# A hand-ordered four-layer graph network on one core: all engines' step orders and PSUM banks laid out anew

## The chip, the cores and the metric

The kernel runs on one core of a Trainium2 chip. The core has a matrix engine (TensorE, "PE" in the profile, with its weight loads on a line of their own, "PEld"), VectorE (DVE), ScalarE (ACT), GpSimd (POOL) and SyncE (SP, which here only issues DMAs). They run apart from each other and meet at semaphores. TensorE writes its results only to PSUM, which has 8 banks of 512 fp32 columns per partition; the other engines read them from there. The metric is device microseconds of one execution of the whole program, as a median over runs.

## The reference

x is 32 graphs of 512 nodes with 128 features, adj one 512x512 0/1 matrix for all of them. Four layers follow each other, each on a normalised and clipped input, and each added to x:

```python
h = jnp.maximum(_layernorm(x, axis=-1), 0.0)
x = x + _L0_gnn_ref(h, adj, ...)     # attention from a fixed pairing of nodes, softmax over axis 1, + h @ self_weight
h = jnp.maximum(_layernorm(x, axis=-1), 0.0)
x = x + _L1_gnn_ref(h, adj, ...)     # attention, layernorm, adj @ h, MLP with layernorm, residual, relu
h = jnp.maximum(_layernorm(x, axis=-1), 0.0)
x = x + _L2_gnn_ref(h, adj, ...)     # attention, + bias, elu
h = jnp.maximum(_layernorm(x, axis=-1), 0.0)
x = x + _L3_gnn_ref(h, adj, ...)     # softmax(edge values) @ h W1, the diagonal @ h W0, + bias
```

An attention of layers 1 and 2 is softmax over the neighbours of leaky_relu(s_i + t_j), and then a product with the features. Everything is fp32. The 32 graphs do not depend on each other; layer 3's 512x512 matrix is made once, from adj.

## The kernel before

**Tiling.** The 32 graphs are taken two at a time: 16 groups, numbered 0 to 15, in the kernel's tables 0 to 9 and a to f. A group's x is 128 partitions x 8 rows x 128. Six slots (NS = 6) hold the buffers of the groups in flight; group g uses slot g modulo 6. A setup block loads weights and adj, and an own chain of twelve "prep" steps (table name g) makes layer 3's matrix while the first groups run.

**Steps.** The table STEPS cuts the work of a group into 55 steps, and says for each how many PSUM tiles it opens and which engines have a part in it. One layer goes round the engines in a long loop: `stat` (VectorE takes the layernorm statistics, L1143; GpSimd makes 1/sqrt of them, L1066 to L1081), `scale` (ScalarE applies it, eight instructions of L921), `norm` (TensorE turns the rows, L634; ScalarE moves them out of PSUM into HT, L914 or L912), and then the layer's products. The steps that the texts below speak of:

- `norm0`, `coef0`, `cmax0`, `coefb0`, `feat0`, `agg0`, `self0`: layer 0. `coef0` is the group of narrow products with wcols; `feat0` the products with Wo.
- `feat1`, `top1`, `spread1a/b`, `att1a/b`: layer 1's features, the maximum turned through TensorE (L732, read by VectorE L1260), the row factors spread through TensorE (L741, from ScalarE's CE, L944), and the attention product (VectorE makes PT, L1280; TensorE multiplies it with HE). The same steps with a 2 are layer 2's; `sums2` is a small product beside them.
- `gin1`, `mlpa1`, `mlpb1`, `mlpc1`: the product with adj, the two MLP products and the layernorm between them. After `mlpc1` VectorE makes the new x (L1311, L1315).
- `elu2`: layer 2's end. `norm3`, `feat3`, `agg3`: layer 3, whose result goes out by DMA.

**What sets the order.** No engine chooses anything when the program runs. The table TURNS holds one string for each engine: each character is a group, and that group's next step on this engine stands next. The function `walk` emits them in that order:

```python
for e, turns in TURNS.items():
    todo = [(name for name, _, engines in steps if e in engines.split()) for steps in [STEPS] * GROUPS + [PREP]]
    order[e] = [(int(g, GROUPS + 1), next(todo[int(g, GROUPS + 1)])) for g in turns]
```

So an engine that comes to a step whose input isn't there waits, and all steps behind it wait with it. The table HOMES gives, in TensorE's order, the bank of each PSUM tile that a step opens (895 of them):

```python
for g, name in order["pe"]:
    for n in range(tiles_of[name]):
        bank = int(next(home))
        tile_at[name, g, n] = bank, opened[bank]
```

TensorE opens a tile only when the one before it in that bank has been read (`open_tile`, semaphore `taken`); the readers wait for `full`. The inner content of each step is fixed. TensorE has 471 steps in its string, VectorE 472, ScalarE 404, GpSimd 144, SyncE 32 loads and stores.

Of the kernel before, what the change touches and what calls it, by code (L numbers as in the profile page):

```python
# [118 lines left out]
    ("eturn", 4, "pe act dve"),  # L119
]  # L120
TURNS = {
    "pe": ("gggggg1021000011201022110g20000001311324331121103024422341401035224121020004300330021112135013332111"
           "5024504434422225432142223163551434333563353325644226755645534446446344563578866776566547648847555855"
           "565576988a9a999777857877a68758865997887696666aa66687897abb9a8bb9989976777776776b899888ba88b889cc977c"
           "c7b9889999c9899dbbccbbdaabcedbec9cdcc9ceed9bcbddfeaafbbeaaeddfcdfddecbdbbbfdbbebbeaffcddeecafbbefdfb"
           "ffcecccdccffcdceeadddafddfeddcaceffacaaeaaeeaeafdeedeedffaffafffeaeefff"),
    "act": ("gg01201200g11002g00301102344110011530223011224010141510022300032421301231201102233103342544322153224"
           "46132314463434553334722346255744365534445583646558566574496645765685556a5869a79875877566977a58877769"
           "88766668897867a8bb88996b79976777a689978b99888ac99c8777b9889b8c999cdd9bbecbceaab99cc9dbbcedbbcffbbeca"
           "caddbecddeafbcdbbbcdfabdadeedcfdbbfabdecffdceccceaffddefceefaddefdfaccdeffcadeeaaafeeefdadeaafffaefe"  # L130
           "efff"),
    "dve": ("g0g12gggg100000102111002g111g00300422501123211022013334304212134410403224311002403400223000112335113"
           "1110322305441644225553222422133544155273433363355633424255866644546664554433457496678665576477468756"
           "58a5855558776888599997777aa889758877669995b8667668a8a666a6897a9b7aab99889777767799bbb67889bc88bb7888"
           "998c77c899d9cc899c9eb9bcccbada9bdebcccc9ebb9dddfbcdddeeeaabcbeeefcafddddacbbffbbedfabbbedfdffbeedccb"
           "afffbeccfddccfeeccfcedfdcaadddfdddeecaffcaaaeaeaeedaaeeedffeffaffffeeaff"),
    "pool": ("012001102134502231043140324102032511653435247234668356594475678a87895569a76987ba867a896bb9cb77988cdc"
           "ec99bddfbecedbeafcdffbbdcaedfeaccfdefdaaeeff"),
    "sp": ("102354061728394a5b6c7d8e9fbcdeaf"),
}  # L140
HOMES = ("0123456701234567012345670125634701254637542601375401430751430051430571426573014303014265742654276534"
         "2703142657203165410365471203654715240365402713617543062175435473535470621062130547210631054726310572"
         "6310573141057341703535326264170532170654321706543706521064375210640641375264026402640264026401375261"
         "3761524037615261403765240314031765231407652314310765210761076152076152431531024224531052376410524371"
         "6052437160541603703754167037272720372037524160375160537124605371242453712736045162730451645451654165"
         "4162730162730162730301627301627301630154623701375460123754601234760513476205132040432510432325104327"
         "6105432761207651423075075076570142365736501426501420650627350736250723560516474207542160754235342160"
         "7416241076262641057324612461246120547631542073616157432061574342061576123547546102735410276413502764"
         "1354135410273641573641502020273641502152150736421642156073421560734215607347340215671340256713456713"
         "450")  # L150


def bcast(ap, n):
# [14 lines left out]
def gnn_kernel(nc, x, adj, Wo_d, Ws_d, att0_d, Wp_d, bp_d, asrc_d, adst_d, gatg_d, gatb_d, eps_d, W1_d, b1_d,  # L168
# [12 lines left out]
    with ctx:  # L181
# [61 lines left out]
        tile_at, mat_at, mat_of = {}, {}, []  # L243
        opened, home = [0] * BANKS, iter(HOMES)
        for g, name in order["pe"]:
# [1266 lines left out]
```

How the kernel before makes its waits and increments, by code:

```python
            @block.sync  # L428
            def _(sp):
                for t in range(T):
                    sp.dma_start(adj_raw[:, t, :], adj[t * P:(t + 1) * P, :]).then_inc(adj_loaded, 16)
                for dst, src in LOADS[0::2]:
                    sp.dma_start(dst, src).then_inc(loaded, 16)
                for s in range(NS // 2):
                    for b in range(G):
                        sp.dma_start(X[s][:, b::G, :],
                                     x.rearrange("b (t p) f -> b p t f", p=P)[s * G + b]).then_inc(x_loaded[s], 16)
                for s in taken:
                    sp.sem_inc(s, 1)
                for s in sig["stored"]:
                    sp.sem_inc(s, 16)
                sp.wait_ge(loaded, 16 * len(LOADS[0::2]))
# [1 line left out]
            @block.gpsimd  # L445
            def _(pool):
                nc.gpsimd.memset(ident[:], 0.0).then_inc(made["pool"], 1)
                nc.gpsimd.memset(ones[:], 1.0).then_inc(made["pool"], 1)
                nc.gpsimd.memset(work1[:], 1.0).then_inc(made["pool"], 1)
                nc.gpsimd.memset(minus_half[:], -0.5).then_inc(made["pool"], 1)
                nc.gpsimd.memset(ones_r[:].bitcast(F32), 1.0).then_inc(made["pool"], 1)
                pool.wait_ge(made["pool"], 5)
                nc.gpsimd.affine_select(out=ident[:], in_=ident[:], compare_op=ALU.not_equal, fill=1.0, base=0,
                                        pattern=[[-1, P]], channel_multiplier=1).then_inc(made["pool"], 1)
```

## Time and profile before

| | |
|---|---|
| median of 3 runs | 1142.54 us (1142.05 to 1143.92) |
| profiled execution, its own time | 1142.13 us |
| its span in the trace | 1140.1 us, 21695 instructions |
| TensorE matmuls busy | 1012.0 us, 89% of the span |
| TensorE weight loads busy | 959.3 us, 84% |
| VectorE busy | 862.8 us, 76% |
| ScalarE busy | 632.3 us, 55% |
| GpSimd busy | 473.3 us, 42% |
| mean granted clock of TensorE | 0.94 of full |
| DMA | 20.20 MB, 18 GB/s on average |

Busy time is the time in which an engine had an instruction under way. TensorE's matmuls overlap, so their time is no measure of how many would fit; the weight loads on their own line say more about that. A bracket behind an instruction of the timeline is the idle time of its engine just before it, and who ended it. The granted clock is one of two levels, 1.0 (2.4 GHz) and 0.5 (1.2 GHz); a value between them is a mean over a stretch.

### The profile page before, as it was taken

What the parts mean: (1) busy time and instruction counts of PE and PEld (TensorE: products, weight loads), DVE (VectorE), ACT (ScalarE), POOL (GpSimd) and SP (SyncE); (2) the same over time, 40 slices, a digit from 0 to 9 for tenths busy, and PEclk for the clock granted to TensorE, in tenths of its full rate; (3) what the DMA queues carried; (4) which work ended last, traced back from release to release, by engine and by line L of the source; (5) the groups of instructions that cost most, each with busy time, mean ns of one, the idle gap of its engine ahead of it and who ended that gap; (6) DMA issues with size and microseconds to landing.
All of it is one profiled execution on the core that took longest, in us unless ns stands there. A gap on an engine that the chain in (4) does not pass through costs nothing. (4 is left out here: it accounts for less than half of the span.)

```text
span 1140.1 us, 21695 instructions
## 1 busy us (share of the span) xinstructions
PE 1012.0 (89%) x7611; PEld 959.3 (84%) x7611; DVE 862.8 (76%) x2536; ACT 632.3 (55%) x1647; POOL 473.3 (42%) x1134
## 2 busy tenths in 40 slices
PE   2597899989899989899999999899999989898997
PEld 2586788979798889889888989789989989888986
DVE  3769777876877668688686988859678876787874
ACT  1053667665565655463645685564655656667352
POOL 2123543643354334443425551633345344546132
PEclk7688799999999889899799999899999999999999
DMA  5000100000101010110001001011010000000001
GB/s 127 1 1 1 56 1 2 1 1 1 37 2 38 1 38 1 38 38 1 1 1 38 1 2 39 1 38 38 1 38 1 1 1 19 2 1 20 2 19 56
DMA packets 38491, 20.20 MB, mean 18 GB/s; under 512 B 3184, under 2 KB 37872, under 8 KB 38384
## 3 DMA queue, kind: packets, MB, share of 16 engines
q1 hardware_dynamic: 36512, 18.42, 5.8%
q8 instruction: 61, 1.00, 0.4%
q10 hardware_dynamic: 1872, 0.40, 0.2%
q14 instruction: 46, 0.38, 0.1%
HBM read 10.43 MB, written 8.39 MB: 17 GB/s over the span
## 5 line engine op out<-in xcount | busy, mean ns | idle before, releaser
L617 PE MATMUL ps<-HE,PT 128*128 128x129 f32 x2048 | 261.2, 280 | 6.0 <-issue 5.0
L617 PEld LDWEIGHTS ps<-HE,PT 128*128 128x128 f32 x2048 | 247.7, 196 | 7.6 <-issue 6.8
L921 ACT ACTIVATE Y<-X,SM 128x128 f32<-128x128 f32 x512 | 203.3, 489 | 54.1 <-POOL SM L1081 54.0
L1280 DVE SCALAR_TENSOR_TENSOR PT<-ps,CE,maskT 128x512 f32<-128x512 f32 x256 | 174.2, 743 | 46.0 <-PE ps L741 39.9
L1066 POOL TENSOR_TENSOR SM<-ST 128x8 f32<-128x8 f32 x96 | 25.9, 270 | 380.0 <-DVE ST L1143 380.0
L1077 POOL TENSOR_TENSOR SM<-SM,minus_half 128x8 f32<-128x8 f32 x96 | 164.6, 1714 | 7.6
L617 PE MATMUL ps<-W,HT 128*128 128x128 f32 (+1 forms) x768 | 133.7, 324 | 3.4 <-ACT HT L914 3.1
L617 PEld LDWEIGHTS ps<-W,HT 128*128 128x128 f32 x768 | 121.4, 202 | 14.8 <-ACT HT L914 4.0
L1143 DVE BATCH_NORM_STATS2 ST<-X 128x6 f32<-128x128 f32 x512 | 104.6, 278 | 17.4 <-DMA X<-in_x_dram 14.8
L634 PE MATMUL ps<-ident,Y 128*128 128x128 f32 x640 | 85.5, 280 | 18.2 <-ACT Y L921 17.5
L634 PEld LDWEIGHTS ps<-ident,Y 128*128 128x128 f32 x640 | 73.2, 145 | 22.2 <-ACT Y L921 20.2
L914 ACT ACTIVATE HT<-ps 128x512 f32<-128x512 f32 x96 | 52.1, 600 | 58.8 <-PE ps L634 58.7
L1098 POOL TENSOR_TENSOR LOWB<-HE,HIB 128x1024 fp32r<-128x1024 f32 x16 | 36.4, 2276 | 110.1 <-ACT HIB L938 110.1
L617 PE MATMUL ps<-HI,a_hi 128*128 128x256 f32 x256 | 74.2, 290 | 4.5 <-DVE LOW L1447 4.5
L617 PE MATMUL ps<-HI,a_lo 128*128 128x256 f32 x256 | 72.8, 284 | 0.0
L617 PE MATMUL ps<-LOW,a_hi 128*128 128x256 f32 x256 | 72.6, 284 | 0.0
L955 ACT ACTIVATE HE<-ps,HE 128x128 f32<-128x128 f32 x256 | 68.9, 380 | 0.0
L617 PE MATMUL ps<-gin_hi,LOW 128*128 128x512 f32 x128 | 57.8, 452 | 3.8 <-DVE LOW L1299 2.7
L1103 POOL TENSOR_TENSOR X<-X,bias 128x1024 f32<-128x1024 f32 x16 | 38.5, 2409 | 54.4 <-ACT Y L921 54.4
L921 ACT ACTIVATE HE<-Y,SM 128x128 f32<-128x128 f32 x128 | 51.1, 492 | 16.5 <-POOL SM L1081 16.4
L921 ACT ACTIVATE Y<-Y,SM 128x128 f32<-128x128 f32 x128 | 51.1, 497 | 12.1 <-POOL SM L1081 12.1
L1143 DVE BATCH_NORM_STATS2 ST<-Y 128x6 f32<-128x128 f32 x256 | 51.7, 275 | 5.7 <-ACT Y L986 5.0
(265 smaller groups left out, 2385.4 us busy)
## 6 DMA issues: line engine op xcount, KB each, us to landing
X<-in_x_dram SPq DMA_DIRECT2D x32, 256.0 KB, 3.4
out_dram<-X SPq DMA_DIRECT2D x32, 256.0 KB, 2.8
adj_raw<-in_adj_dram SPq DMA_DIRECT2D x4, 256.0 KB, 3.8
W<-in_L_gnn_W_dram SPq DMA_DIRECT2D x1, 128.0 KB, 4.3
Ws<-n_L_gnn_self_weight_dram ACTq DMA_DIRECT2D x1, 64.0 KB, 3.4
W<-in_L_gnn_W_dram ACTq DMA_DIRECT2D x1, 64.0 KB, 3.8
feat2w<-in_L_gnn_W_dram ACTq DMA_DIRECT2D x1, 64.0 KB, 4.4
Wo<-L_gnn_others_weight_dram SPq DMA_DIRECT2D x1, 64.0 KB, 4.6
```

The lines of the kernel that those rows point to most:

```text
L617: return nc.tensor.matmul(o, w, m, start=start, stop=stop, skip_group_check=True)
L634: mm = T_(o[:, t * P:(t + 1) * P], Y[s][:, t * G + b, 0:F], ident[:])
L914: a = A(HT[s][:, b, :], o, ACT.Relu)
L921: a = A(dst[:, n, 0:F], src[:, n, 0:F], func, scale=SM[s][:, S_RSTD, n:n + 1], bias=SM[s][:, S_SHIFT, n:n + 1])
L955: a = A(HE[s][:, k, 0:F], o[:, 2 * P * b:2 * P * b + F], ACT.Identity, scale=HE[s][:, k, F:F + 1])
L1066: TT(sm[:, S_DIF, :], st[:, :, 1], st[:, :, 4], ALU.subtract)
L1077: link(TT(sm[:, S_RSTD, :], sm[:, S_VAR, :], minus_half[:], ALU.pow))
L1098: TT(LOB[s], VA[s], HIB[:].bitcast(F32), ALU.subtract).then_inc(sig["by_pool"][s], 1)
L1103: TT(X[s][:], X[s][:], repeat(bias3[:], TG), ALU.add).then_inc(sig["by_pool"][s], 1)
L1143: a = V.bn_stats(ST[s][:, n, :], src(n))
L1280: a = V.scalar_tensor_tensor(out=PT[r][:, j, :], in0=o, scalar=CE[s][:, c:c + 1], in1=maskT[:, j, :].bitcast(F32), op0=ALU.max, op1=ALU.mult)
```

## The change

Only the two tables are new: TURNS (the order of the steps on each engine) and HOMES (the bank of each tile). The steps, their contents, their instructions, the buffers and all waits that follow from the data stay; a wait for a bank follows its new neighbour. On TensorE 342 of 471 steps stand at another place, by 1.7 places on average and by 15 at most; on VectorE 352 of 472 (1.6 on average, at most 10), on ScalarE 299 of 404, on GpSimd 78 of 144, and 9 of the 32 loads and stores. TensorE's first eight steps and the last three are the same. The diff (cut; the rows of both tables are all replaced in this manner):

```diff
 TURNS = {
-    "pe": ("gggggg1021000011201022110g20000001311324331121103024422341401035224121020004300330021112135013332111"
+    "pe": ("gggggg1001001021120011g20002020010131231213341103420224434101032421520120030400300323123113151311125"
...
-    "sp": ("102354061728394a5b6c7d8e9fbcdeaf"),
+    "sp": ("135024061728394a5b6c7d8e9fadbcef"),
 }
-HOMES = ("0123456701234567012345670125634701254637542601375401430751430051430571426573014303014265742654276534"
+HOMES = ("0123456701234567012345670123456710456273410627341056267234105467235726435107210764325107643762435763"
...
```

**TensorE, layer 2 of group 6.** The rows below are `feat2` (feat2w,HT), `sums2` (feat2w,HS), `top2` (ident,MX), `spread2a` and `spread2b` (ident,CE) of group 6, with steps of other groups between them. Before:

```order
L634 MATMUL ps<-ident,Y 128x128 x16
L617 MATMUL ps<-feat2w,HT 128x130 x8
L617 MATMUL ps<-feat2w,HS 128x128 x2
L732 MATMUL ps<-ident,MX 128x128 x2
L741 MATMUL ps<-ident,CE 128x128 x4
L617 MATMUL ps<-Wo,HT 128x128 x8
L617 MATMUL ps<-CS,adj_top 128x4 x8
L741 MATMUL ps<-ident,CE 128x128 x4
```

And now, the same place (bias,pick and W,HT are `mlpa1` of group 7):

```order
L617 MATMUL ps<-feat2w,HT 128x130 x8
L617 MATMUL ps<-feat2w,HS 128x128 x2
L732 MATMUL ps<-ident,MX 128x128 x2
L617 MATMUL ps<-bias,pick 128x512
L617 MATMUL ps<-W,HT 128x128 x4
L617 MATMUL ps<-bias,pick 128x512
L617 MATMUL ps<-W,HT 128x128 x4
L741 MATMUL ps<-ident,CE 128x128 x8
```

`spread2a` stood right behind `top2`; now the MLP step of another group stands between them.

**TensorE, layer 0 of groups 9 and 10.** The rows are `norm0` (ident,Y), `coef0` (wcols,HT), `cmax0` (ident,MX) and `feat0` (Wo,HT), the first row the end of group 8's `self0`. Before:

```order
L617 MATMUL ps<-Ws,HT 128x128 x4
L634 MATMUL ps<-ident,Y 128x128 x8
L617 MATMUL ps<-wcols,HT 128x4 x16
L725 MATMUL ps<-ident,MX 128x128 x2
L617 MATMUL ps<-Wo,HT 128x128 x8
```

And now:

```order
L617 MATMUL ps<-Ws,HT 128x128 x4
L617 MATMUL ps<-wcols,HT 128x4 x8
L634 MATMUL ps<-ident,Y 128x128 x8
L725 MATMUL ps<-ident,MX 128x128 x2
L634 MATMUL ps<-ident,Y 128x128 x8
L617 MATMUL ps<-Wo,HT 128x128 x8
L617 MATMUL ps<-wcols,HT 128x4 x8
```

The two groups' `coef0`, 16 narrow products in a row before, stand apart.

**VectorE, behind `mlpc1` of group 7.** L1315 is the last instruction of `mlpc1`, which makes the group's new x; the L1143 on X that belongs to it is `stat2` of the same group. Before:

```order
L1311 SCALAR_TENSOR_TENSOR Y<-HE,ps 128x4x128 x2
L1315 SCALAR_TENSOR_TENSOR X<-Y,X 128x1024
L1224 SCALAR_TENSOR_TENSOR X<-ps,CE,X 128x128 x8
L1260 TENSOR_REDUCE MX<-ps 128x2
L1264 TENSOR_TENSOR CF<-DS,MX 128x8
L1266 TENSOR_SCALAR CF<-DS,MX 128x4 x2
L1155 COPY US<-ps 128x32
L1158 COPY CD<-US 128x8
L1159 TENSOR_TENSOR CD<-US 128x4
L1161 SCALAR_TENSOR_TENSOR CD<-CD 128x12
L1163 TENSOR_REDUCE MX<-CD 128x2
L1143 BN_STATS ST<-X 128x6 x8
```

And now:

```order
L1311 SCALAR_TENSOR_TENSOR Y<-HE,ps 128x4x128 x2
L1315 SCALAR_TENSOR_TENSOR X<-Y,X 128x1024
L1143 BN_STATS ST<-X 128x6 x8
L1280 SCALAR_TENSOR_TENSOR PT<-ps,CE,maskT 128x512 x4
L1143 BN_STATS ST<-Y 128x6 x8
L1280 SCALAR_TENSOR_TENSOR PT<-ps,CE,maskT 128x512 x4
L1224 SCALAR_TENSOR_TENSOR X<-ps,CE,X 128x128 x8
```

The statistics stand right behind the new x; three steps of other groups that stood between them (`agg0`, `top1`, `coef0`) have gone to other places.

## Rows read from the trace of the kernel before

**Rows 1.** The page, busy time of the engines (us, share of span, instructions).

```profile
PE 1012.0 (89%) x7611; PEld 959.3 (84%) x7611; DVE 862.8 (76%) x2536; ACT 632.3 (55%) x1647; POOL 473.3 (42%) x1134
```

**Rows 2.** Busy time by stretch: length, engines with instructions, granted clock, DMA share, GB/s.

```profile
0.00:38.60 38.60, 7.75 (x31) 6.91 (x31) 19.52 (x70) 5.63 (x7) 7.92 (x14) 0.71 0.44 94
38.60:68.00 29.40, 26.97 (x108) 22.73 (x109) 18.19 (x54) 12.46 (x30) 10.87 (x30) 0.74 0.00 1
68.00:1140.00 1072.00, 977.33 (x7473) 929.65 (x7471) 825.12 (x2414) 614.18 (x1611) 454.50 (x1090) 0.95 0.05 15
```

**Rows 3.** Waits of TensorE from 68 us on: total us, times, longest.

```profile
PE ps L634 <- ACT Y L921: 17.5, 11, 6.1
PE ps L741 <- ACT CE L944: 11.5, 10, 1.4
PE ps L732 <- DVE MX L1254: 11.3, 15, 2.1
PE ps L617 <- ACT HT L914: 7.6, 9, 1.2
PE ps L617 <- ACT HT L912: 4.6, 4, 1.5
PE ps L617 <- DVE LOW L1299: 2.7, 3, 1.8
```

**Rows 4.** Timeline of TensorE, steps that stood right behind their source: start, us, instruction.

```profile
127.27 7.92 PE L617 MATMUL ps<-HE,PT 128*128 128x129 f32 x46 [3.04 <-issue]
...
392.07 0.47 PE L617 MATMUL ps<-bias,pick 128*128 128x512 f32 x1 [1.15 <-ACT HT L910]
...
506.23 2.02 PE L617 MATMUL ps<-feat2w,HT 128*128 128x130 f32 x16 [0.96 <-ACT HT L912]
...
618.30 0.65 PE L741 MATMUL ps<-ident,CE 128*128 128x128 f32 x4 [1.33 <-ACT CE L944]
...
736.36 5.38 PE L617 MATMUL ps<-W,HT 128*128 128x256 f32 x16 [0.78 <-ACT HT L914]
...
781.98 0.43 PE L732 MATMUL ps<-ident,MX 128*128 128x128 f32 x2 [0.46 <-DVE MX L1254]
```

**Rows 5.** Timeline of TensorE, `feat0` at half and at full clock.

```profile
547.95 3.62 PE L617 MATMUL ps<-Wo,HT 128*128 128x128 f32 x16
...
618.79 1.95 PE L617 MATMUL ps<-Wo,HT 128*128 128x128 f32 x16
```

**Rows 6.** Busy time by stretch, the two `coef0` of groups 9 and 10 and after.

```profile
545.60:559.20 13.60, 12.87 (x60) 12.50 (x61) 6.62 (x29) 8.92 (x24) 7.76 (x23) 0.50 0.00 0
559.20:600.00 40.80, 38.11 (x290) 34.89 (x289) 31.46 (x84) 21.01 (x58) 14.73 (x38) 1.00 0.01 2
```

**Rows 7.** Timeline, group 7 from `mlpc1` to `norm2`, all engines.

```profile
642.58 1.05 PE L617 MATMUL ps<-W,HT 128*128 128x128 f32 x8
...
646.69 1.23 DVE L1315 SCALAR_TENSOR_TENSOR X<-Y,X 128x1024 f32<-128x1024 f32 x1
647.95 2.29 DVE L1224 SCALAR_TENSOR_TENSOR X<-ps,CE,X 128x128 f32<-128x128 f32 x8
...
652.04 1.64 DVE L1143 BATCH_NORM_STATS2 ST<-X 128x6 f32<-128x128 f32 x8
...
659.14 3.21 ACT L921 ACTIVATE Y<-X,SM 128x128 f32<-128x128 f32 x8
...
662.42 3.21 ACT L921 ACTIVATE Y<-X,SM 128x128 f32<-128x128 f32 x8
...
668.53 0.71 PE L634 MATMUL ps<-ident,Y 128*128 128x128 f32 x5
```

**Rows 8.** Timeline of GpSimd, the power instruction twice.

```profile
646.69 2.75 POOL L1077 TENSOR_TENSOR SM<-SM,minus_half 128x8 f32<-128x8 f32 x1
...
651.78 1.68 POOL L1077 TENSOR_TENSOR SM<-SM,minus_half 128x8 f32<-128x8 f32 x1
```

**Rows 9.** The page, the group of the power instruction (mean in ns of one).

```profile
L1077 POOL TENSOR_TENSOR SM<-SM,minus_half 128x8 f32<-128x8 f32 x96 | 164.6, 1714 | 7.6
```

More of the change, by code:

```diff
@@ L121 @@
 TURNS = {
-    "pe": ("gggggg1021000011201022110g20000001311324331121103024422341401035224121020004300330021112135013332111"
[L123 to L130, printed above, removed]
-           "efff"),
[L132 to L136, printed above, removed]
@@ L137 @@
-    "pool": ("012001102134502231043140324102032511653435247234668356594475678a87895569a76987ba867a896bb9cb77988cdc"
-           "ec99bddfbecedbeafcdffbbdcaedfeaccfdefdaaeeff"),
-    "sp": ("102354061728394a5b6c7d8e9fbcdeaf"),
-}
-HOMES = ("0123456701234567012345670125634701254637542601375401430751430051430571426573014303014265742654276534"
[L142 to L150, printed above, removed]
@@ new lines @@
+    "pe": ("gggggg1001001021120011g20002020010131231213341103420224434101032421520120030400300323123113151311125"
+           "4020404324422425235422213135513633453463533643524526625457345446443644565368676865647757846457555988"
+           "5655576889a979a9877a57877878659865988676667669aa668b9b978799aa979b878677b7767b7869888988bb88a9c79cb7"
+           "cc7898999cb99899cdbcbdaebbcadbc9cecac9dd9cebcbadeedfbabeefdadbdcdebdbcfbdbbffdebbaeffcedcdafbefbfefe"
+           "cfbdcccdcfcfccdadeddeddfafeddecfacfaaaceadeaeeaeeafdffefedaffafefeaefff"),
@@ new lines @@
+    "act": ("gg0110201g2010g0200101320311404015132023012142010141102503203100220321321311243021400332442532422345"
+           "13123146334635454334246235524743736554443585645565866454674965758695655568a67a7988577a59687765877686"
+           "89766679887b86ba7899679879867b77698987b98898ac7989cb7a7b8989c8999cd9debbecbc9abad9cc9bbcedbcbfbbefdc"
+           "bdaacebddceabcfbbdadfcdbadeecdfbfdbabfecedcfdccefcaefddcafefddedfeefcafdcafcdaeaeadeeeffdfaffeaaaeef"
+           "efff"),
+    "dve": ("g12g0gggg0011001010100g121g2010030242215102312102031334302214143410043232114020400202303033412101115"
+           "3112023435410442262355242252133545543123433635673544233562566844564466545443534666768795574867747565"
+           "685a558558778889956a9977a78798758696758799b8666768a8a66699ab677989aaa97b87876779bb976778b8c89b8bb888"
+           "899c7c7899ccdb9899ce9c9bccb9dabadccbc9edb9bceddfacbdeaddeebbeeecfcdaddbdfbacbffdbbaefbdbedfffbcceefb"
+           "fdfeafbccddcecfccecdcfdfeddaafddeddecafacaefeaaeeadafafeeeeffdaffffeefaf"),
@@ new lines @@
+    "pool": ("120010102132405231304103412240032513156435422674386536547495678a878956a5796987ba6789b68ba7c97b898ccd"
+           "ec9d9bedfbcdebeafcfdfbbcdeadfecafcdefdaeaeff"),
+    "sp": ("135024061728394a5b6c7d8e9fadbcef"),
+}
+HOMES = ("0123456701234567012345670123456710456273410627341056267234105467235726435107210764325107643762435763"
+         "2471605320547146057132460571324163167243167240524052430167526752675674230156715674230542637105423710"
+         "5423716130754230617615764230764230157642031576420315764215767036703670421561356135615361750426175325"
+         "3613761304250425761034253425342537615034276742150376124576103576035716024731560601512473547360541273"
+         "6054127360451260457345126047303470370370531264317026574031572640263157402316457026341571571450721634"
+         "5340721653402170217026534065342065201734652065201736420517364207364732051632407512407512407070512643"
+         "2436243636243627405135165136513652740427136541365036503764150372645021645163701263701237645014052376"
+         "1452054250437612506123742374237504621375042137163507142614261426142635104726372632651074263510742634"
+         "2364251074326514307265143075126430751075107264531031725604316072543416130472651472630514307265143075"
+         "143")
```

## The prediction

> **What bounds the kernel now.** I read the busy times first: TensorE's matmuls 89% of the span, its weight loads 84%, VectorE 76%, ScalarE 55% [rows 1]. Then the same by stretch [rows 2]. Up to 38.6 us the setup runs, and from there to 68 us TensorE does prep work in an order that the change leaves alone. The change can act on the remaining 1072 us only. There TensorE has 977.3 us of matmuls, so it is idle for 94.7 us, at a mean granted clock of 0.95; VectorE is busy for 825.1 us, 77%. TensorE is the bound in the middle, but it waits about 9% of the time. The waits [rows 3] are of two sorts. Short ones: the step that stands next on TensorE needs what VectorE or ScalarE makes of the step just before (CE from L944, MX from L1254, HT from L914 and L912). Long ones: the first product of a new layer (L634 behind ACT Y L921) comes before the loop through VectorE, GpSimd and ScalarE is round; 17.5 us in 11 waits. The chain that ends last is made of TensorE's work and of these waits, so whatever is taken from them is taken from the time, as long as nothing else comes late.
>
> By a rule of the Trainium skill (Perfetto Trace Analysis, Identifying the Most-Contended Engine) matmul time overstates how full TensorE is, and weight load time says it better. The trace has 929.7 us of weight loads in the 1072 [rows 2], so by the rule the room is 142 us and not 95; the sum below doesn't use it.
>
> **The change, part by part.** No instruction is added or removed, so nothing has to be priced but order. I price it by neighbours on TensorE.
>
> *Short round trips.* For each pair of steps of one group in which the second needs the answer of another engine to the first, I take the shortest idle time that the trace shows with nothing between them: top to spread 1.33 us, mlpb1 to mlpc1 1.15, norm2 to feat2 0.96, norm3 to feat3 0.78, feat1 to top1 0.46, spread to attention about 3.0 [rows 4]; the others (feat3 to agg3, norm0 to coef0, coef0 to cmax0, gin1 to mlpa1 and so on) are read in the same way. Against it stands the TensorE work between the two in either order, each step at the shortest time that it took in the trace. Where the work is shorter than the trip, TensorE must wait for the difference. Counting places that lack at least 0.25 us:
>
> before there are 54 with 48.6 us in all, after there are 17 with 12.2 us. The largest items: top2 to spread2a 6 places and 7.1 us, then none; spread to attention 7 and 6.9 us, then 4 and 3.0; feat1 to top1 9 and 4.1 us, then 3 and 1.4; mlpb1 to mlpc1 3 and 3.4 us, then none; norm3 to feat3 4 and 3.1 us, then 1 and 0.8; norm2 to feat2 3 and 2.9 us, then none. Group 6 shows how: its spread2a waited 1.33 us behind top2 [rows 4], and now mlpa1 of group 7 stands between, whose two tiles take longer than that (a later mlpc1 half, 8 matmul records of the same form, takes 1.05 us [rows 7]). The waits bear the count out: those of the short sort by L944, L1254, L914 and L912 alone come to 35.0 us [rows 3]. The difference is 36.4 us; about 1.4 us of it I count twice (coefb0 is followed by both agg0 and self0), so −35. Lower end: half of it, −18, if the step put between is itself late as often as not; upper end −36.
>
> *Long loops.* Five trips go through three engines: self0 to norm1, att1b to gin1, mlpa1 to mlpb1, mlpc1 to norm2, att2b to norm3. By the same count with the shortest loop of each kind they lack 27.4 us before and 30.7 after, so +3.3 as one end. But most loops were longer than the shortest. With each group's own loop of before, up to the end of the ScalarE or VectorE instruction that TensorE waits for, the 80 loops lack 175 us before and 256 after: the new order brings their ends 81 us closer in all. Group 7's mlpc1 to norm2 is the plainest. Its loop was 22.0 us long: mlpc1 ends at 643.6 [rows 7], the last L921 of scale2 at 665.6, and TensorE began norm2 at 668.53. Now only 10.7 us of TensorE work stand between. The other engines' orders are changed to suit. On VectorE three steps of other groups stood between L1315, which ended at 647.9, and the statistics at 652.04 (4.1 us); they are gone from there. On ScalarE scale2 ran at 662.42 behind another scale [rows 7]; that one stays. So this loop falls to about 18 us, and lacks 7 of them. Such a shortage is not a wait of the same size, since the groups of six slots are in flight and delay each other's steps only once: in the trace 175 us of shortage go with 17.5 + 2.7 = 20.2 us of waits [rows 3], which makes +9 of the 81; divided by six groups in flight it makes +14. I take +14, the dearer, because group 7 keeps 7 us. Other end: half of 81, +40.
>
> *Clock.* At half clock the 16 matmuls of feat0 take 3.62 us, at full 1.95 [rows 5], so 46% of such a time is lost. With 0.95 over 1072 us [rows 2] some 107 us run at half, and 107 x 0.91 x 0.46 is 45 us. The longest stretch, 13.6 us, lies behind the two coef0 in a row of groups 9 and 10 [rows 6], and these stand apart now. Others followed TensorE's idle places. But the long waits will make new ones, so I take a tenth of the 45, −4; ends 0 and −15.
>
> *Banks.* A tile now waits for another tile's reader. In the order before, a twentieth of the tiles were opened within 0.85 us of work behind the tile before them in the bank; in the new one within 1.54. No wait of before names a bank with more than 1 us, so the gain is put at nothing (ends 0 and −2), covered by other waits at the same places. The loads and stores that moved are nothing: 9 of 32, and SyncE is idle in between.
>
> *Sum.* Own time of the profiled execution 1142.1; −35 + 14 − 4 = −25 gives 1117.1. The median is 0.4 above the profiled time, so 1117.5.
>
> **The rivals.**
>
> 1. *The loops get shorter too.* If VectorE and ScalarE run everywhere as behind mlpc1 of group 7, the long term is +3.3 and the clock gives −15: −36 + 3 − 15 = −48, 1094. For it: both engines have room (77% and 57% of the 1072 us [rows 2]), and the tables of all engines were changed together. Against: a loop that lacks 7 us.
>
> 2. *The waits only move.* TensorE finds its next input sooner, but VectorE in its fixed order is late instead, and the short gains end in front of the next step. Then 1141. For it: VectorE is at 77%, and a late step there holds whatever stands behind it. Against: the waits on VectorE's L1254 and L1299 are under 2.2 us each [rows 3].
>
> 3. *Slower: the tight loops.* If the loops keep their length and each group's lateness holds up the next, the long term is half of the 81, +40.5; with −35 and no clock gain that is +5.5, 1148. It decides from the point where the long term passes 35 + 2.3. It would show first at norm2 of group 7 (10.7 us for a loop of 22.0) and at gin1 of group 6. For it: the sum is real and has nothing to hide it but idle room of others. Against: 175 us of shortage cost only 20 before.
>
> 4. *GpSimd is held up.* The power instruction took 1.68 us mostly and 2.75 when it met VectorE work [rows 8], 1.07 more. A new order has new meetings. If each of the 96 rstd chains met one, 96 x 1.07 / 6 in flight is +17 over the forecast: 1134. But the mean of all 96 power instructions is 1.71 [rows 9], so few of them meet anything now, and I give it little.
> The Trainium skill (SBUF — State Buffer, Who interferes with whom) has the rule behind such a case: VectorE with two inputs in SBUF and GpSimd share one pair of ports, and the one that comes second waits for the whole instruction. The trace agrees by that 1.07 us.
>
> **How the numbers follow.** Forecast 58% (1107 to 1130), rival 1 20%, rival 2 7%, rival 3 9%, rival 4 6%. The range of 8 in 10 reaches from 1095, which takes in half of rival 1 and a little more, to 1141, which leaves out rival 3 and a part of rival 2. About 0.2% (2.3 us) is what can be told from no change here. Faster by more: forecast, rival 1, rival 4 and a little less, 0.83. Within: most of rival 2, 0.07. Slower: rival 3 and the rest, 0.10.
>
> **What would show it.** In the changed profile, TensorE's waits on L944, L1254, L914 and L912 should fall from 35.0 to about 10 us, and spread2a of group 6 should start without an idle time. TensorE's waits on ACT Y L921 should rise from 17.5 to some 30. The idle time behind 68 us should go from 94.7 to about 73, and the granted clock stay at 0.95 or rise a little. Matmul durations at full clock must be the same. I am wrong if the short waits stay above 25 us (then the steps put between are late themselves), if L921 waits pass 50 us (rival 3), or if the clock alone moves the time by more than 15 us.

## The result, and the profile after

The kernel after takes 1085.06 us (median of 4 runs, 1079.57 to 1088.0) against 1143.23 for the kernel before beside it: 0.9479 of its time, 95% interval 0.9431 to 0.9526. The forecast was 1117.5 us with a range of 1095 to 1141. The direction was right; the gain is more than twice the size, 58 us for a forecast 25.

The profiled execution took 1079.57 us, the fastest of the four; its span is 1077.8. Busy times of the page, the answer to [rows 1]:

```profile
PE 985.5 (91%) x7611; PEld 940.4 (87%) x7611; DVE 857.4 (80%) x2536; ACT 634.1 (59%) x1647; POOL 482.6 (45%) x1134
```

The same by stretch, the answer to [rows 2] (length, then TensorE, its weight loads, VectorE, ScalarE, GpSimd, the granted clock, DMA share, GB/s):

```profile
0.00:38.60 38.60, 7.76 (x31) 6.92 (x31) 19.14 (x67) 5.63 (x7) 7.92 (x14) 0.71 0.53 94
38.60:68.00 29.40, 26.16 (x106) 22.00 (x107) 18.27 (x56) 9.87 (x22) 10.40 (x30) 0.74 0.00 1
68.00:1077.80 1009.80, 951.57 (x7476) 911.53 (x7474) 820.02 (x2415) 618.60 (x1618) 464.25 (x1090) 0.97 0.06 16
```

All of it is behind 68 us: that part fell from 1072.0 to 1009.8, by 62.2 us. It splits in two. Idle TensorE time went from 94.7 to 58.2 (−36.5). Matmul time went from 977.3 to 951.6 (−25.8), with the same instructions. This second part the forecast had at 4 us.

The waits of TensorE from 68 us on (total us, times, longest), the answer to [rows 3]:

```profile
PE ps L634 <- ACT Y L921: 14.9, 12, 3.6
PE ps L617 <- ACT HT L914: 4.7, 5, 1.8
PE ps L732 <- DVE MX L1254: 4.1, 6, 1.6
PE ps L741 <- ACT CE L944: 2.7, 4, 1.4
...
PE ps L617 <- ACT HT L912: 1.2, 1, 1.2
...
PE ps L617 <- DVE LOW L1299: 0.8, 2, 0.5
```

The four short ones (L944, L1254, L914, L912) fell from 35.0 to 12.7 us, close to the 10 of the forecast. The long one behind L921 should have risen to 30 and fell from 17.5 to 14.9.

Group 6 on TensorE, the answer to the fourth row of [rows 4]: behind `top2` (ident,MX) stands `mlpa1` of group 7, and `spread2a` (ident,CE) starts without idle time. The step put between waits 0.52 us itself, so 0.8 of the 1.33 us are won here.

```profile
574.87 0.43 PE L732 MATMUL ps<-ident,MX 128*128 128x128 f32 x2
575.83 0.47 PE L617 MATMUL ps<-bias,pick 128*128 128x512 f32 x1 [0.52 <-ACT HT L981]
576.14 1.05 PE L617 MATMUL ps<-W,HT 128*128 128x128 f32 x8
576.95 0.48 PE L617 MATMUL ps<-bias,pick 128*128 128x512 f32 x1
577.27 1.05 PE L617 MATMUL ps<-W,HT 128*128 128x128 f32 x8
578.16 1.04 PE L741 MATMUL ps<-ident,CE 128*128 128x128 f32 x8
```

Group 7 from `mlpc1` to `norm2`, the answer to [rows 7]:

```profile
606.90 1.05 PE L617 MATMUL ps<-W,HT 128*128 128x128 f32 x8
607.75 1.39 DVE L1311 SCALAR_TENSOR_TENSOR Y<-HE,ps 128x512 f32<-128x512 f32 x2
609.18 1.23 DVE L1315 SCALAR_TENSOR_TENSOR X<-Y,X 128x1024 f32<-128x1024 f32 x1
610.44 1.65 DVE L1143 BATCH_NORM_STATS2 ST<-X 128x6 f32<-128x128 f32 x8
...
616.59 0.20 POOL L1081 TENSOR_TENSOR SM<-SM 128x8 f32<-128x8 f32 x1
616.82 3.19 ACT L921 ACTIVATE Y<-X,SM 128x128 f32<-128x128 f32 x8 [0.78 <-POOL SM L1081]
...
620.07 1.09 PE L634 MATMUL ps<-ident,Y 128*128 128x128 f32 x8 [1.12 <-ACT Y L921]
```

`mlpc1` ended at 607.95, `norm2` began 12.1 us later; before it was 24.9. The statistics start 0.03 us behind the new x instead of 4.1. From the end of `mlpc1` to the end of `scale2` this loop takes 12.1 us (607.95 to 620.01), where the forecast gave it 18. `scale2` still follows another group's scale on ScalarE, as the forecast said, but that one (612.86 to 616.05, `scale3` of group 6) is done before this group's factors are ready, and costs it nothing. Against the 10.7 us of TensorE work between, a loop of 12.1 lacks 1.4, and the wait is 1.12: the forecast's way of counting holds here, its length of the loop does not.

At full clock matmuls take what they took: the 16 of `feat0` 1.95 us, as in [rows 5]. What is new is how long the clock is full. From the trace's records of the granted clock TensorE ran at half for 99.0 us before, and for 51.2 after, from 68 us to its last matmul. Both are of one execution each, and this time varies from one execution to the next: the mean granted clock lay between 0.934 and 0.961 in 19 runs of the kernel before, and between 0.948 and 0.967 in the 4 of the kernel after. The page's group of the power instruction, the answer to [rows 9], hardly moved (1714 to 1699 ns):

```profile
L1077 POOL TENSOR_TENSOR SM<-SM,minus_half 128x8 f32<-128x8 f32 x96 | 163.1, 1699 | 7.6
```

### The profile page after: what moved, and what is told of

Same layout as the page of the kernel before. It is cut to its first block and busy times, and to the rows that moved or that the text cites. A ratio compares the mean times of both kernels' runs of the same rounds, so it can differ in the third digit from the quotient of the medians.

```text
span 1077.8 us, 21695 instructions
## 1 busy us (share of the span) xinstructions
PE 985.5 (91%) x7611; PEld 940.4 (87%) x7611; DVE 857.4 (80%) x2536; ACT 634.1 (59%) x1647; POOL 482.6 (45%) x1134
## 5 line engine op out<-in xcount | busy, mean ns | idle before, releaser
L617 PE MATMUL ps<-HE,PT 128*128 128x129 f32 x2048 | 257.5, 277 | 2.1 <-issue 1.6
L617 PEld LDWEIGHTS ps<-HE,PT 128*128 128x128 f32 x2048 | 243.8, 193 | 3.0 <-issue 2.4
L921 ACT ACTIVATE Y<-X,SM 128x128 f32<-128x128 f32 x512 | 203.5, 485 | 70.7 <-POOL SM L1081 70.6
L1066 POOL TENSOR_TENSOR SM<-ST 128x8 f32<-128x8 f32 x96 | 23.7, 247 | 336.8 <-DVE ST L1143 336.6
L1077 POOL TENSOR_TENSOR SM<-SM,minus_half 128x8 f32<-128x8 f32 x96 | 163.1, 1699 | 7.6
L617 PE MATMUL ps<-W,HT 128*128 128x128 f32 (+1 forms) x768 | 127.1, 313 | 0.8 <-ACT HT L914 0.8
L617 PEld LDWEIGHTS ps<-W,HT 128*128 128x128 f32 x768 | 116.1, 194 | 10.4 <-ACT HT L914 1.0
L1143 DVE BATCH_NORM_STATS2 ST<-X 128x6 f32<-128x128 f32 x512 | 104.7, 278 | 5.2 <-DMA X<-in_x_dram 2.2
L634 PE MATMUL ps<-ident,Y 128*128 128x128 f32 x640 | 86.4, 282 | 15.4 <-ACT Y L921 14.9
L634 PEld LDWEIGHTS ps<-ident,Y 128*128 128x128 f32 x640 | 74.2, 146 | 19.4 <-ACT Y L921 17.9
L921 ACT ACTIVATE HE<-Y,SM 128x128 f32<-128x128 f32 x128 | 51.1, 486 | 25.8 <-POOL SM L1081 25.8
L914 ACT ACTIVATE HT<-ps 128x512 f32<-128x512 f32 x96 | 51.5, 595 | 22.8 <-PE ps L634 22.4
L921 ACT ACTIVATE Y<-Y,SM 128x128 f32<-128x128 f32 x128 | 51.0, 490 | 15.9 <-POOL SM L1081 15.9
L1143 DVE BATCH_NORM_STATS2 ST<-Y 128x6 f32<-128x128 f32 x256 | 51.5, 274 | 9.8 <-ACT Y L986 8.9
L617 PEld LDWEIGHTS ps<-HI,a_hi 128*128 128x128 f32 x256 | 48.6, 190 | 4.1 <-DVE LOW L1447 3.2
```

What stands on the lines that cost most here:

```text
L617: return nc.tensor.matmul(o, w, m, start=start, stop=stop, skip_group_check=True)
L634: mm = T_(o[:, t * P:(t + 1) * P], Y[s][:, t * G + b, 0:F], ident[:])
L914: a = A(HT[s][:, b, :], o, ACT.Relu)
L921: a = A(dst[:, n, 0:F], src[:, n, 0:F], func, scale=SM[s][:, S_RSTD, n:n + 1], bias=SM[s][:, S_SHIFT, n:n + 1])
L1066: TT(sm[:, S_DIF, :], st[:, :, 1], st[:, :, 4], ALU.subtract)
L1077: link(TT(sm[:, S_RSTD, :], sm[:, S_VAR, :], minus_half[:], ALU.pow))
```

## The experiments

Every kernel differs from before or after in TURNS and HOMES alone. The obvious halves (the new order on one engine, the old on the others) can't be run: an order carries the others' in it, and in such a mix each engine stands at a step that waits for one further down on another. So the experiments start from a whole order and change a part, the banks laid out anew to match in each of them. Waits and busy times are those of one profiled execution; where that one is far from the median, it is said.

**The short places filled, the rest as before.** 87 steps of TensorE's string moved. By the prediction's count the short shortages fall from 48.7 to 27.3 us. One place (TensorE, layer 1; `top1` moved back behind half an attention product):

```diff
-L732 MATMUL ps<-ident,MX 128x128 x2
 L617 MATMUL ps<-SR,norow 128x129
 L617 MATMUL ps<-HE,PT 128x129 x4
...
+L732 MATMUL ps<-ident,MX 128x128 x2
```

> The order of before, with TensorE's string alone changed at 87 places so that steps of other groups stand in the short round trips (top to spread, mlpb1 to mlpc1, feat1 to top1 and so on); the strings of VectorE, ScalarE, GpSimd and SyncE are those of before, and the long loops lack as much as before. By the count of the prediction the short trips lack 27.3 us at 34 places instead of 48.7 at 54, so 21.4 less. Theory S (the recorded one: the gain of the change is in the short trips of TensorE's own order): 1143 - 21 and some 3 to 5 of clock, 1115 to 1124, ratio 0.975 to 0.983. Theory L (a wait that is taken from TensorE comes back at the next input that is late, as long as the other engines' order is the old one): 1138 to 1146, ratio 0.996 to 1.003.

Measured: 1146.4 us, 1.0021 of before [1.0002, 1.0041]. A count that is 21 us better bought nothing. The waits:

```profile
PE ps L634 <- ACT Y L921: 18.0, 14, 3.6
PE ps L732 <- DVE MX L1254: 12.4, 14, 3.4
...
PE ps L741 <- ACT CE L944: 8.4, 8, 1.4
```

That on L944 fell by 3.1 us against [rows 3], those on L1254 and L921 rose by 1.1 and 0.5, and TensorE's idle time behind 68 us is 97.8 against 94.7. VectorE and ScalarE still come to their steps in the old order, and so at the old time.

**The other engines' orders new, TensorE's as before.** VectorE, ScalarE and GpSimd have an order made from before's by exchanges, and the banks are new.

```diff
-    "dve": ("g0g12gggg100000102111002g111g00300422501123211022013334304212134410403224311002403400223000112335113"
+    "dve": ("g102ggggg001000120111020g11g100300224011235231102021333404213124414002332140102403032020004112335113"
```

> The order of before with TensorE's string untouched and only VectorE's, ScalarE's and GpSimd's strings laid out anew (not those of the change, which can't be joined with the old TensorE string; new ones by exchanges that bring the inputs of TensorE earlier), banks given anew. TensorE's short trips lack 48.7 us at 54 places as before. Theory S: no gain, 1138 to 1146. Theory L: the waits of TensorE hang on how early the loops through the other engines end, so a good part of the change's 58 us comes without moving a step on TensorE: 1095 to 1115, and ACT Y L921 and the other waits of TensorE fall together.

Measured: 1130.03 us, 0.9859 [0.9799, 0.992]. This is between the two ranges expected. The four runs reach from 1117.63 to 1132.68, and the profiled one is the 1117.63; its row in the table below is that of a run 12 us better than the median.

**TensorE's order new, the others' as before.** The counterpart, 188 steps moved.

```diff
-    "pe": ("gggggg1021000011201022110g20000001311324331121103024422341401035224121020004300330021112135013332111"
+    "pe": ("gggggg20110010020110211g0022000003111324311321103420244231401032254112020004303000321112153013332111"
```

> The order of before with TensorE's string alone laid out anew by exchanges that shorten the whole (not those that lessen the short trips: these lack 50.5 us at 53 places, as before 48.7 at 54); VectorE, ScalarE and GpSimd as before. Theory S: nothing or a little slower, 1140 to 1150. Theory L (each engine's string alone can win a little, both together much more): 1125 to 1137, less than the others alone gave in the second experiment or about as much, and the two far from adding up to the change's 58 us.

Measured: 1141.3 us, 0.9991 [0.9963, 1.002], no gain, and not the 1125 to 1137 of theory L. The profiled run, 1148.55, is the slowest of ten. So TensorE's order alone gave 0% and the others' alone 1.4%, where the change of all together gives 5.2%. These are orders of their own and not halves of the change, and a better one for either side alone may exist. But the count of neighbours had nothing to say about it: the order of the others alone has the same TensorE string as before, so its count is 48.7 to the last digit, and it won 12 us.

**The short places taken back in the kernel after.** 53 steps of TensorE's string moved, nothing else. The count rises from 12.2 to 33.9 us. Group 7's place:

```diff
 L732 MATMUL ps<-ident,MX 128x128 x2
-L617 MATMUL ps<-Wo,HT 128x128 x8
-L741 MATMUL ps<-ident,CE 128x128 x8
+L741 MATMUL ps<-ident,CE 128x128 x4
+L617 MATMUL ps<-Wo,HT 128x128 x8
+L741 MATMUL ps<-ident,CE 128x128 x4
```

> The changed kernel with TensorE's top2 put right behind sums2, spread2a right behind top2 and mlpc1 right behind mlpb1 where at most two steps stood between them and it can be done; all other strings as in the change. By the count the short trips lack 33.9 us at 35 places instead of 12.2 at 17, so 21.7 more; the long loops lack 1.6 less. Theory S: 1085 + 22 and 3 to 5 of clock, 1107 to 1112. Theory L: an early step on TensorE that waits also holds everything behind it, for engines whose order expects the step later, so a wait costs more than its own length: 1120 to 1140.

Measured: 1135.84 us, 0.9958 of before [0.9932, 0.9984], so 51 us over the kernel after: 2.3 us for each one of the count, where the filled places above gave 0. The waits:

```profile
PE ps L741 <- ACT CE L944: 26.7, 13, 6.1
PE ps L732 <- DVE MX L1254: 13.8, 10, 4.5
PE ps L617 <- ACT HT L910: 11.0, 8, 2.2
PE ps L634 <- ACT Y L921: 6.4, 10, 1.5
```

The waits on L944 and L1254 are now much longer than the shortest trip. The timeline of VectorE, TensorE and ScalarE at group 7 shows why:

```profile
642.67 1.40 DVE L1311 SCALAR_TENSOR_TENSOR Y<-HE,ps 128x512 f32<-128x512 f32 x2
...
643.49 0.40 PE L732 MATMUL ps<-ident,MX 128*128 128x128 f32 x2
...
644.11 1.26 DVE L1315 SCALAR_TENSOR_TENSOR X<-Y,X 128x1024 f32<-128x1024 f32 x1
645.40 0.42 DVE L1260 TENSOR_REDUCE MX<-ps 128x2 f32<-128x256 f32 x1
645.86 2.32 DVE L1264 TENSOR_TENSOR CF<-DS,MX 128x8 f32<-128x8 f32 x1
648.10 0.35 DVE L1266 TENSOR_SCALAR CF<-DS,MX 128x4 f32<-128x4 f32 x2
...
648.85 1.12 PE L741 MATMUL ps<-ident,CE 128*128 128x128 f32 x4 [4.95 <-ACT CE L944]
```

TensorE had its `top2` done at 643.9. VectorE was in the middle of `mlpc1` of another group, as its string says, and took the maximum at 645.4. From there to CE it was 3.2 us, of which 2.32 went into one tiny instruction (last section). TensorE waited 4.95 us where [rows 4] shows 1.33 for the same trip. Of the 4.95, about 1.5 is VectorE's lateness, 2.15 what that instruction took over its usual 0.17, and 1.33 the trip. The price of a place is set by where the other engine stands in its own string, and by what it meets there; 1.33 is only its floor. The runs show that these 53 moved steps cost 51 us (theory L had 1120 to 1140); that all of it comes in this way is argued from this one place.

**The statistics late.** In the kernel after, on VectorE alone, 14 of the 16 `stat2` moved behind two steps of other groups:

```diff
 L1315 SCALAR_TENSOR_TENSOR X<-Y,X 128x1024
-L1143 BN_STATS ST<-X 128x6 x8
 L1224 SCALAR_TENSOR_TENSOR X<-ps,CE,X 128x128 x8
 L1251 COPY DS<-ps 128x4 x4
 L1254 TENSOR_REDUCE MX<-DS 128x2
+L1143 BN_STATS ST<-X 128x6 x8
```

> The changed kernel with one step moved on VectorE in 14 of 16 groups: stat2, which stood at most two places behind mlpc1 of its group, stands two places further back (two steps of other groups go first); all other strings as in the change. Each of these loops mlpc1 to norm2 gets about two VectorE steps longer, some 3 to 5 us, 40 to 70 us over the 14. Theory P (the price in the prediction: a ninth to a sixth of a loop's lengthening becomes a wait): +5 to +12, 1090 to 1097. Theory L (loops stand in the chain that decides, and TensorE has nothing in front of the next late input): +25 to +45 us, 1110 to 1130, and ACT Y L921 grows from 14.9 us to over 30.

Measured: 1134.81 us, 0.9923 of before [0.9898, 0.9948], 50 us over the kernel after. No TensorE step has moved. The waits of TensorE:

```profile
PE ps L634 <- ACT Y L921: 37.2, 16, 8.8
```

From the new x to the end of the statistics it takes 8.4 us instead of 2.9, as a mean of 16 groups: 16 x 5.5 = 88 us of lengthening, and 50 us of time, 0.57 for one, more than either range expected. The prediction priced such lateness at 14/81 = 0.17, but as waits for a microsecond of shortage. In the two traces the wait on L921 rose by 22.3 us, other idle time of TensorE by 13.0, and its matmul time by 16.2 (half clock 99.0 against 51.2).

**Other banks under the order of after.** TURNS is that of the kernel after, HOMES is laid out anew.

```diff
-HOMES = ("0123456701234567012345670123456710456273410627341056267234105467235726435107210764325107643762435763"
+HOMES = ("0123456701234567012345670123456710452634710263471052623647105723645273645102710236457102364523647523"
...
```

> The changed kernel with its orders kept and only the banks given anew: each tile takes the bank whose last tile is expected to be read first. 732 of 895 tiles get another bank. If the banks are worth nothing beyond not being in the way (the prediction): 1081 to 1091, the same within 0.3%. If the change's bank table carries a part of the gain by itself: 1092 or more.

Measured: 1084.06 us, 0.9478 [0.9447, 0.9509]: the kernel after, to 1 us. Banks are worth nothing here, as forecast.

**Narrow products in pairs.** In the kernel after the two `coef0` of neighbouring groups put behind each other at three places, 21 steps of TensorE moved:

```diff
-L617 MATMUL ps<-wcols,HT 128x4 x8
-L634 MATMUL ps<-ident,Y 128x128 x8
+L634 MATMUL ps<-ident,Y 128x128 x8
+L617 MATMUL ps<-wcols,HT 128x4 x16
 L725 MATMUL ps<-ident,MX 128x128 x2
 L634 MATMUL ps<-ident,Y 128x128 x8
 L617 MATMUL ps<-Wo,HT 128x128 x8
-L617 MATMUL ps<-wcols,HT 128x4 x8
```

> The changed kernel with TensorE's coef0 of groups 7 and 8, of 9 and 10, and of 13 and 14 put next to each other again (the wcols products, 4 columns each, 32 in a row); the rest of all strings as in the change. If the narrow products alone bring the half clock, without an idle place: stretches of 7 to 14 us at half clock at the three places, where the change has 3.4 us at two of them and none at the third, so 15 to 25 us more at half clock and +8 to +14 us: 1093 to 1099. If the half clock comes only behind idle places: no more than 51 us at half clock as before, 1083 to 1089.

Measured: 1094.35 us, 0.9562 [0.9547, 0.9577], 9.3 over the kernel after and inside the range that was expected if the narrow products bring the half clock. Half clock went from 51.2 to 71.7 us. The 9.3 us are not all the clock: against the kernel with other banks (profiled at 1084.23, half clock 61.4) matmul time is 4.3 us more and idle time 6.2. (The trace writes two records for each of these fp32 products: the x16 of the order are 32 there.) The three pairs (stretches; the last number but two is the clock):

```profile
440.00:450.20 10.20, 10.20 (x50) 10.20 (x50) 6.42 (x18) 5.38 (x13) 0.37 (x2) 0.50 0.10 31
515.10:525.30 10.20, 9.27 (x45) 9.30 (x45) 4.66 (x26) 4.89 (x14) 4.46 (x17) 0.50 0.00 0
754.00:760.80 6.80, 6.80 (x33) 6.80 (x33) 4.25 (x20) 3.21 (x8) 5.62 (x14) 0.50 0.01 4
```

The first has an idle time of 1.34 us shortly before it, the second one of 2.27 between its halves. The third is the clean one. TensorE has no idle time in front of it from 745 us on, and the clock falls inside the 32 narrow products:

```profile
748.00:751.00 3.00, 3.00 (x29) 3.00 (x28) 2.81 (x8) 2.68 (x12) 0.00 (x0) 1.00 0.00 0
751.00:753.00 2.00, 2.00 (x20) 2.00 (x18) 2.00 (x9) 1.40 (x4) 0.35 (x3) 1.00 0.00 0
753.00:754.00 1.00, 1.00 (x11) 1.00 (x10) 1.00 (x3) 0.00 (x0) 0.79 (x5) 1.00 0.00 0
754.00:755.00 1.00, 1.00 (x7) 1.00 (x7) 1.00 (x2) 0.00 (x0) 0.84 (x3) 0.50 0.00 0
```

By the Trainium skill (TensorE: Matmul & The Clock Gate, Part 1) the clock follows how busy TensorE has been. The profile's busy time doesn't tell it here: TensorE has work under way in every microsecond from 748 to 754 us and falls to half all the same, so a full row of busy time is no promise of the full clock.

**All engines further in the same direction.** If the gain comes from the orders of all engines together, more such exchanges should find more. The strings of TensorE, VectorE, ScalarE and GpSimd and the banks are new; the first row of TensorE's:

```diff
-    "pe": ("gggggg1001001021120011g20002020010131231213341103420224434101032421520120030400300323123113151311125"
+    "pe": ("gg01010010g11g0gg012212g0002200010132131123314304015423320420214122050003100215303433013131142112551"
```

> All strings laid out further from those of the change by the same sort of exchanges. The short trips lack 6.2 us at 6 places (changed kernel 12.2 at 17), the long loops 23.0 (30.8). Theory S: 1085 - 6 and a little clock, 1075 to 1080. Theory L (all engines' orders together, long loops included): 1040 to 1060, with TensorE's idle time behind 68 us under 30 us and at most 25 us at half clock.

Measured: 1056.62 us, 0.9238 of before [0.9208, 0.9268]. It beats both kernels, the one after by 28 us. The time is in the range of theory L; idle time (51.5 us, not under 30) and half clock (30.7, not 25) are not. Its stretch behind 68 us:

```profile
68.00:1051.80 983.80, 932.32 (x7419) 896.73 (x7418) 836.11 (x2396) 612.41 (x1610) 469.08 (x1082) 0.98 0.06 17
```

30.7 us at half clock are left there. All 7611 matmul records are in this trace as in the others; 57 more of them than after stand before 68 us, so a part of the 19.3 us less matmul time is work done earlier. Over the whole span the matmuls take 970.2 us against 985.5 after and 1012.0 before.

## Why the prediction was right and wrong

The columns are worked out from the windows behind 68 us and the clock records of each trace up to the last matmul. A break is an idle time of TensorE over 0.02 us. Each row is one execution; after and banks, which are worth the same, show how much that is: 10 us at half clock.

| kernel | length | matmuls busy | idle | at half clock | breaks |
|---|---|---|---|---|---|
| before | 1072.1 | 977.3 | 94.8 | 99.0 | 103 |
| after | 1009.8 | 951.6 | 58.2 | 51.2 | 74 |
| short places filled | 1076.2 | 978.4 | 97.8 | 99.0 | 104 |
| others' orders | 1047.6 | 961.5 | 86.1 | 75.1 | 90 |
| TensorE's order | 1078.6 | 980.2 | 98.4 | 105.8 | 109 |
| short places back | 1064.0 | 963.3 | 100.7 | 75.1 | 96 |
| statistics late | 1061.3 | 967.8 | 93.5 | 99.0 | 72 |
| banks | 1014.4 | 954.8 | 59.6 | 61.4 | 73 |
| narrow pairs | 1024.8 | 959.1 | 65.7 | 71.7 | 73 |
| further | 983.8 | 932.3 | 51.5 | 30.7 | 46 |

**Short round trips, −35.** Right as a size: TensorE's idle time outside the waits on L921 and L1299 fell from 74.5 to 42.5, by 32, and the four named waits from 35.0 to 12.7. Wrong as a mechanism of its own. The same count made 21 better brought 0, and 22 worse cost 51. The term came out in the change, where the other engines' orders moved with it.

**Long loops, +14. This is the step that failed first**: "the new order brings their ends 81 us closer", priced as a loss. It measured −4.5 (L921 and L1299, 20.2 to 15.7). In the table, from the end of the step before to the start of the norm, as means of 16 groups in us; in brackets how much of it had passed when the scale was done, which is the loop's own length. The last column is the prediction's count of all 80 loops made again from each trace, with the loops of that trace (it gives 178 for the prediction's 175 before, and 260 for its 256 with the old loops in the new order).

| kernel | self0 to norm1 | mlpc1 to norm2 | att2b to norm3 | shortage |
|---|---|---|---|---|
| before | 24.1 (17.8) | 21.7 (17.6) | 33.3 (29.3) | 178 |
| after | 20.9 (18.5) | 17.8 (15.2) | 30.2 (27.1) | 110 |
| short places filled | 24.4 (17.7) | 22.5 (17.7) | 33.2 (29.3) | 183 |
| others' orders | 23.7 (19.1) | 21.3 (17.1) | 31.8 (27.6) | 123 |
| TensorE's order | 24.4 (17.4) | 21.6 (17.5) | 32.9 (29.0) | 176 |
| short places back | 22.2 (19.4) | 21.4 (18.0) | 32.5 (28.1) | 154 |
| statistics late | 22.5 (19.9) | 21.4 (19.0) | 31.9 (28.2) | 220 |
| further | 27.1 (19.5) | 17.0 (15.3) | 33.9 (30.4) | 80 |

The ends came 3.4 us closer on average. Of this only 1.3 are shorter loops (the first kind even got longer); 2.2 are time in which a norm's input lay ready. What the prediction had wrong is that each group keeps its own loop. The new strings make short the loops that have little work between their ends: the shortage fell from 178 to 110 us, where the forecast raised it to 256. What went out is ScalarE's queue in front of the scale (from the power instruction's end to the scale's start 3.5 us before and 1.8 after, on average); on VectorE the wait between new x and statistics, 4.1 us at group 7, is 0.7 on average before and 1.3 after, so group 7 was no fair sample of it. The price per microsecond of shortage was about right: L921 and L1299 together took 0.11 of it before, 0.14 after, 0.17 with late statistics.

The shortage of the loops alone doesn't order the kernels either. With the others' orders it is nearly that of after, but the short trips lack 48.7 us and TensorE is idle for 86.1; with the short places filled they lack 27.3, the loops 183, and it is idle for 97.8; with late statistics 12.2 and 220, and it is idle for 93.5. Only where both are small is the idle time small: 58.2 after, 51.5 further. That one gain needs the other is a reading of these rows, in which more than the two counts moved.

**Clock, −4.** Right in sign, too small, as far as one execution of each kernel tells. It measured 47.8 us less at half clock, which at 0.34 us of matmul time each is −16. The 0.34 and the next figure are fitted: matmul time = 951.6 + 0.34 x (half clock − 51.2) + 0.3 x (breaks − 74) gives the nine traces from before to "narrow pairs" within 3 us ("further" it puts at 936.2, 3.9 too high). "Banks" and "statistics late" carry the clock part alone (61.4 and 99.0 us, 72 and 73 breaks): 955.1 and 967.9 by the fit, 954.8 and 967.8 measured. By it, 29 breaks fewer give another −9 that the prediction had not. It took the idle time as the whole room; a break costs a little of the busy time around it too. That this is the filling and emptying of TensorE's pipeline is an argument, not shown.

**The sum** in the prediction's terms: −32 − 4.5 − 16 − 9 = −61.5, where the profiled executions differ by 62.6 (the medians by 58.2). Against the forecast's −25 that is 18.5 from the loops, 12 from the clock and 9 from the breaks, less 3 from the short trips.

**The rivals.** Rival 1 (loops shorter too, 1094) came nearest, and with the breaks added it would have given 1085. It had 20%. Its mechanism is half of what happened: the loops got little shorter, but those that the new order leaves little time for did. Its evidence against was one loop, group 7's, given 18 us where it took 12.1. Rivals 2 and 3 are refuted by waits of 12.7 and 14.9 us; but rival 2 is what the first experiment shows, where the other engines keep their old order. Rival 4 is refuted by a mean of 1699 ns for the power instruction.

**The tests named beforehand.** Short waits about 10: 12.7. Group 6 without idle: yes. Idle 73: 58.2. L921 to 30: 14.9. The clock alone under 15 us: it passed it slightly.

What stays open is how the 58 us split between the engines. What each side's order gave alone (0 and 12 us) doesn't add up to it, and no half of the change runs.

## What to carry to other kernels

Where orders are fixed on all engines, the distance between two steps on the busiest engine says nothing by itself: follow the answer through the other engines' strings, in the same new order, before pricing it. When producers and consumers move together, don't carry a loop's length over from the old order: work out for each group where its steps stand in the new strings, and only then compare the loop with the work between its ends. Count matmul time as movable too; here it fell by 26 of 62 us with the same instructions, which the fit gives to the clock and to fewer breaks.

## What the runs showed of the hardware

- **Narrow products bring the clock down without any idle time.** 32 records of 4 columns in a row took TensorE from 1.0 to 0.5 (2.4 to 1.2 GHz) at 754 us, with 6.00 us of gapless work just before. 16 in a row, apart from others, kept 1.0 while they ran: the rows of the kernel after below took 1.94 and 1.95 us at full clock. They are not safe either. Behind the first of them, and an idle 0.66 us, the clock fell at 514.81 us; and in the kernel with other banks it fell at 518.47 us behind 16 such products and 8 more of 4 columns (`coefb0`), with no idle time.

```profile
511.50 1.94 PE L617 MATMUL ps<-wcols,HT 128*128 128x4 f32 x16
...
519.53 1.95 PE L617 MATMUL ps<-wcols,HT 128*128 128x4 f32 x16
```

- **A GpSimd instruction can hold up VectorE, too.** L1264, 128x8 with two inputs, takes 0.17 to 0.22 us in all 32 cases before. With the places taken back it took 2.32 us once, beside an addition on GpSimd:

```profile
645.82 2.34 POOL L1103 TENSOR_TENSOR X<-X,bias 128x1024 f32<-128x1024 f32 x1
```

  The addition began 0.04 us earlier and took its usual time (its median is 2.36 us in this trace); it ended at 648.16, L1264 at 648.18. The line's own summary (minimum, median and longest in ns) has no such case in the kernel before, and in the kernel after a longest one of 2.02 us:

```profile
L1264 DVE TENSOR_TENSOR CF<-DS,MX x32: 166/167/220, 121.4 to 1090.3; 128x8 f32<-128x8 f32 x32
```

```profile
L1264 DVE TENSOR_TENSOR CF<-DS,MX x32: 166/167/2017, 120.7 to 1017.8; 128x8 f32<-128x8 f32 x32
```

  This is the Trainium skill's rule (SBUF — State Buffer, Who interferes with whom) in the direction that rival 4 had left out: here VectorE comes second and waits for the whole instruction. The trace agrees, with 2.15 us on the path of `spread2a`.
